# Feed-forward's second product in high and low float32r parts, with identity products in TensorE's waits

## What is computed

```python
s = attention(xn)                       # 16 heads, 4 key groups, rotary, window 64 + front 32
gate, up = split(xn @ ternary(w_gate_up).T)      # 1024 wide each
h = silu(gate) * up
g = silu(rms_norm(h) @ ternary(w_proj).T)        # the second product, 1024 -> 256
x = x + (s @ wo) * g
```

## Time and profile before

| | |
|---|---|
| runs | 811.24 us median of 3 (810.93 to 811.31) |
| the profiled execution | 811.08 us; its span, first to last instruction, 809.3 us |
| TensorE | 769.6 us busy (95%), weight loads 474.5 us (59%) |
| VectorE | 597.1 us busy (74%) |
| ScalarE | 475.9 us busy (59%) |
| GpSimd | 299.7 us busy (37%) |
| line 1044, the second product | 256 records, 59.3 us busy |
| mean granted clock of TensorE | 0.993 |

### The profile page before, as it was taken

How to read it: one execution, slowest core, us unless ns; L and a number is a source line. 1 busy time by engine, 2 the same in 40 slices (tenths; PEclk the granted TensorE clock), 3 DMA queues, 4 the chain that set the end, 5 groups by cost and what they waited for, 6 DMA issues and landing times.

```text
span 809.3 us, 13334 instructions
## 1 busy us (share of the span) xinstructions
PE 769.6 (95%) x4656; PEld 474.5 (59%) x4656; DVE 597.1 (74%) x1584; ACT 475.9 (59%) x968; POOL 299.7 (37%) x255
## 2 busy tenths in 40 slices
PE   4978899899999999999999999999999999999996
PEld 2545578555456667846446667856436667865543
DVE  5989886779766766788856677787948677677852
ACT  3898872536867673243777674143795766233582
POOL 1268770411029882002008885002005887100201
PEclk9999999999999999999999999999999999999998
DMA  9311002381013210084004120057002200027300
GB/s 296 102 58 46 1 29 84 124 232 37 3 33 87 60 33 1 1 260 107 2 14 104 33 64 1 1 164 201 3 2 55 79 21 1 1 78 217 73 3 26
DMA packets 56819, 55.37 MB, mean 68 GB/s; under 512 B 14257, under 2 KB 43313, under 8 KB 56753
## 3 DMA queue, kind: packets, MB, share of 16 engines
q1 hardware_dynamic: 52768, 49.63, 21.5%
q10 hardware_dynamic: 3664, 3.84, 1.8%
q0 software_dynamic: 320, 1.05, 0.4%
HBM read 39.00 MB, written 15.24 MB: 67 GB/s over the span
## 4 chain that ended last, share of the span: by engine, by line
PE 68%; issue 12%; DVE 8%; POOL 5%; ACT 4%; DMA 1%; ACTq 0%; POOLq 0%; DVEq 0%
PE bank L933 13%; PE bank L1044 7%; PE bank L1251 6%; PE bank L1235 5%; PE bank L968 5%; PE bank L1030 5%; PE bank L1146 5%; PE bank L1174 4%; PE bank L1218 3%; PE bank L1011 3%; PE bank L979 2%; PE bank L1223 2%; POOL region L597 2%; PE bank L1166 2%; PE bank L993 2%
## 5 line engine op out<-in xcount | busy, mean ns | idle before, releaser
L1612 DVE TENSOR_REDUCE mx<-bank 128x1 f32<-128x512 f32 x256 | 161.2, 684 | 26.2 <-PE bank L1174 22.7
L601 POOL TENSOR_TENSOR region<-region 128x512 f32<-128x512 f32 x75 | 100.3, 1337 | 148.1 <-DVE region L1429 143.4
L933 PE MATMUL bank<-xnT,wrope 128*128 128x512 f32 x320 | 147.8, 605 | 3.9 <-ACT xnT L728 1.9
L885 ACT ACTIVATE region<-bank 128x512 f32<-128x512 f32 x256 | 132.9, 602 | 25.7 <-PE bank L1223 24.3
L761 ACT ACTIVATE region<-region,nb 128x128 f32<-128x128 f32 x256 | 81.5, 390 | 55.9 <-DVE nb L1441 55.6
L933 PEld LDWEIGHTS bank<-xnT,wrope 128*128 128x128 f32 x320 | 58.8, 194 | 66.6 <-issue 61.8
L597 POOL TENSOR_TENSOR region<-region,sin_sb 128x512 f32<-128x512 f32 x60 | 81.5, 1358 | 41.4 <-ACT region L741 40.8
L630 POOL TENSOR_TENSOR region<-region,bo_bc 128x256 f32<-128x256 f32 x16 | 11.6, 727 | 201.1 <-DVE region L1490 201.1
L1422 DVE TENSOR_TENSOR region<-bank,cos_sb 128x512 f32<-128x512 f32 x80 | 54.3, 686 | 35.2 <-PE bank L933 34.9
L739 ACT ACTIVATE region<-bank 64x512 f32<-64x512 f32 x80 | 47.5, 594 | 49.5 <-DVE region L1422 40.0
L968 PE MATMUL bank<-region 128*128 128x128 f32 x512 | 72.2, 285 | 1.9 <-POOL region L601 1.9
(11 more groups left out here) (148 smaller groups left out, 1336.1 us busy)
## 6 DMA issues: line engine op xcount, KB each, us to landing
wrope<-in_wrope SPq DMA_DIRECT2D x80, 128.0 KB, 2.1
scratch<-region SPq DMA_DIRECT2D x16, 512.0 KB, 4.7
Qp<-scratch SPq DMA_DIRECT2D x56, 128.0 KB, 3.4
Kp<-scratch SPq DMA_DIRECT2D x56, 128.0 KB, 3.8
scratch<-region SPq DMA_DIRECT2D x16, 256.0 KB, 5.2
X<-in_x SPq DMA_DIRECT2D x4, 512.0 KB, 4.1
out<-X SPq DMA_DIRECT2D x16, 128.0 KB, 2.1
VW<-v_rows SPq DMA_DIRECT2D x16, 102.0 KB, 2.8
```

Of the source, the lines that this page charges most:

```text
L601: nc.gpsimd.tensor_tensor(dst, dst, tiles(sw[:, r % 2, :], i), ALU.add)\
L885: nc.scalar.activation(P1[:, n % 8, :], turned_bank(n)[:, :], ACT.Exp, scale=SCALE1)\
L933: mm = nc.tensor.matmul(misc(b, name)[:, 0:width], lhs(c), xnT[:, c, :], start=(c == 0), stop=(c == DC - 1))
L1612: nc.vector.tensor_reduce(mx1[:, g % 2, column:column + 1], scores_bank(m)[:, :], AX.X, ALU.max)\
```

## The change

1. `wpT` is float32r. ScalarE writes each row block of `H` rounded into `H_hi` (in `Qp`'s room), VectorE writes the rest, `H - H_hi`, into `H_lo` (in `Kp`'s room). `projected` does two float32r products of 256 columns in the place of each float32 product.
2. For b of 1 to 3 the gate and up jobs all lie in units 0 to 11; `projected(0)` is done in halves in units 14 and 15, the sums of squares come at the head of step 16, `projected(1)` at its end. `projected(2)` precedes the second `turn_outputs0`, `output0(3)` precedes `turn_half(0)`. For b = 0 `projected(0)` now follows the last probabilities instead of standing in step 16.
3. The root and the gate of tile 0 move to VectorE's steps 16 and 17 for b of 1 to 3; the gate of tile 2 comes before the gated attention of tile 0. The sums have a bank of their own.
4. `keep_busy` turns the identity: 30 times before the first norm is there, 8 times before the first rotary jobs, 8 times in units 7 and 11 of b = 0, 4 times before each `turn_half(0)`, 18 times before the last `wo1` products.
5. Raw weights that lay in `wpT` lie in `H` while they are quantised.

```diff
-FFN_LATER = [0, 0, 2, 2, 0, 0, 2, 2, 0, 0, 2, 2, 2, 1, 1, 0]
+FFN_LATER = [1, 1, 2, 2, 0, 1, 2, 2, 0, 1, 2, 2, 0, 0, 0, 0]
+def ups_at(b, s):
+    return [i for kind, i in ffn_at(b, s) if kind == "up"] if 0 <= s < NKV * TT else []
-        wpT = sb("wpT", [P, HC, DIM])
+        wpT = sb("wpT", [P, HC, DIM], F32R)
+        H_hi, H_lo = Qp, Kp
...
+            def high_rows(b, i):
+                act.wait_ge(h_ready.sem, h_ready.at(b, i + 1))
+                nc.scalar.activation(H_hi[:, i, :], H[:, i, :], ACT.Copy).then_inc(hhi_ready.sem, 1)
...
                     if b == 0 and s:
                         first_blocks(b, s - 1)
+                    for i in ups_at(b, s - 1):
+                        high_rows(b, i)
...
+            def keep_busy(dst, n):
+                for _ in range(n):
+                    nc.tensor.transpose(dst[:, 0:P], ident[:, :], ident[:, :])
             pe.wait_ge(ident_loaded, 16)
+            keep_busy(t_bank[0], FILL_START)
...
+                if h == 0:
+                    keep_busy(misc(b, name), 4)
                 pe.wait_ge(xn_ready.sem, xn_ready.at(b, TT + 2 * h + 2))
...
             turn_rows(0)
+            keep_busy(t_bank[0], FILL_UNIT)
             front(0)
...
-                        mm = nc.tensor.matmul(misc(b, ("proj", t))[:, 0:DIM], H[:, c, t * P:(t + 1) * P],
-                                              wpT[:, c, :], start=(c == 0), stop=(c == HC - 1))
+                        if t == 0:
+                            pe.wait_ge(hlo_ready.sem, hlo_ready.at(b, c + 1))
+                        for part in (H_hi, H_lo):
+                            mm = nc.tensor.matmul(misc(b, ("proj", t))[:, 0:DIM], part[:, c, t * P:(t + 1) * P],
+                                                  wpT[:, c, :], start=(c == 0 and part is H_hi),
+                                                  stop=(c == HC - 1 and part is H_lo))
...
-                    if s == NKV * TT:
-                        pe.wait_ge(h_ready.sem, h_ready.at(b, HC))
-                        projected(0)
+                    if b and s == NKV * TT:
+                        square_sums()
...
+                        if b == 0 and s in FILL_UNITS:
+                            keep_busy(t_bank[(s - 1) % 2], FILL_UNIT)
...
+                        if b and s == OT_UNIT - 1:
+                            projected(0, 0, HC // 2)
                         if s == OT_UNIT:
                             turn_outputs0(b, 0)
+                        if b and s == OT_UNIT:
+                            misc_done(projected(0, HC // 2), ("proj", 0))
                     if 1 <= s <= NKV * TT:
                         turn_probs0(b, s - 1)
                     if s >= 2:
                         attend0(b, s - 2)
+                    if b and s == NKV * TT:
+                        misc_done(projected(1), ("proj", 1))
...
-                misc_done(projected(1), ("proj", 1))
-                turn_outputs0(b, 1)
                 pe.wait_ge(pt1_ready.sem, pt1_ready.at(b, NKV * TT))
                 pe.wait_ge(mx0_done.sem, mx0_done.at(b, NKV * TT * REP))
-                projected(2, 0, 2)
+                if b == 0:
+                    misc_done(projected(0), ("proj", 0))
+                    square_sums()
+                    misc_done(projected(1), ("proj", 1))
+                misc_done(projected(2), ("proj", 2))
+                turn_outputs0(b, 1)
+                projected(3, 0, HC // 4)
                 pe.wait_ge(ot_ready.sem, ot_ready.at(b, 2))
                 output0(0)
                 output0(1)
-                misc_done(projected(2, 2), ("proj", 2))
+                misc_done(projected(3, HC // 4), ("proj", 3))
                 output0(2)
-                misc_done(projected(3), ("proj", 3))
+                output0(3)
                 turn_half(b, 0)
-                output0(3)
...
+                if b + 1 == B:
+                    keep_busy(m_bank[2], FILL_END)
                 pe.wait_ge(y_ready.sem, y_ready.at(b, 2))
...
+            def low_rows1(b, i):
+                dve.wait_ge(hhi_ready.sem, hhi_ready.at(b, i + 1))
+                nc.vector.tensor_tensor(H_lo[:, i, :], H[:, i, :], H_hi[:, i, :], ALU.subtract)\
+                    .then_inc(hlo_ready.sem, 1)
...
                     for kind, i in ffn_at(b, s) if s < NKV * TT else ():
                         (gate if kind == "gate" else times_up)(b, i)
+                    for i in ups_at(b, s - 2) if s < NKV * TT else ():
+                        low_rows1(b, i)
                     if b == 0 and s in SPLIT_LOW:
                         split_ffn1(*SPLIT_LOW[s])
```

More of the change, by code:

```diff
@@ L52 @@
 S16 = SEQ // 32
+FILL_START, FILL_UNIT, FILL_END = 30, 8, 18
+FILL_UNITS = (7, 11)
 class Signal:
@@ L71, in misc_jobs @@
         jobs += [("wt", k) for k in TURN_AT.get(s, ())] if b == 0 else []
-    jobs += [("proj", 0), ("proj", 1), ("ot", 1), ("wo0", 0), ("wo0", 1), ("proj", 2), ("wo0", 2), ("proj", 3)]
-    jobs += [("xh", 0), ("wo0", 3), ("xh", 1), ("v1", 0)] + [("qk", j) for j in range(4)] + [("v1", 1)]
+    jobs += [("proj", 0), ("sum", 0), ("proj", 1), ("proj", 2), ("ot", 1), ("wo0", 0), ("wo0", 1), ("proj", 3)]
+    jobs += [("wo0", 2), ("wo0", 3), ("xh", 0), ("xh", 1), ("v1", 0)] + [("qk", j) for j in range(4)] + [("v1", 1)]
     jobs += [("dup", i) for i in range(HC)] + [("mt", 0)] + [("down", t) for t in range(TT)]
@@ L259, in build @@
         x_slot1 = X[:, 1, :, :].rearrange("p t d -> p (t d)")
-        wp_flat = wpT[:, :, :].rearrange("p c n -> p (c n)")
+        h_flat = H[:, :, :].rearrange("p c n -> p (c n)")
+        h_room = [h_flat[:, n * SEQ:n * SEQ + PIECE] for n in (HC - 3, HC - 5)]
         w0_flat, w1_flat = (w[:, :, :, :].rearrange("p k a b -> p (k a b)") for w in (w0T, w1T))
-        raw_room = [x_slot1, th[:, :, :].rearrange("p t n -> p (t n)"), wp_flat[:, 0:PIECE],
-                    wp_flat[:, PIECE:2 * PIECE], x_slot1, wp_flat[:, 0:PIECE]]
+        raw_room = [x_slot1, th[:, :, :].rearrange("p t n -> p (t n)"), h_room[0],
+                    h_room[1], x_slot1, h_room[0]]
         tern_raw = [raw_room[TERN_ORDER.index(i)] for i in range(NPIECE)]
@@ L402, in released @@
                 "proj": lambda: [(g_ready, n + 1)],
+                "sum": lambda: [(fr_step, 2)],
                 "wo0": lambda: [(sg_step, n + 1)],
@@ L1043, in projected, with square_sums @@
                     for c in range(first, last):
-                        mm = nc.tensor.matmul(misc(b, ("proj", t))[:, 0:DIM], H[:, c, t * P:(t + 1) * P],
-                                              wpT[:, c, :], start=(c == 0), stop=(c == HC - 1))
-                    return mm
+                        if t == 0:
[4 more added lines that the diff above has]
+                                                  stop=(c == HC - 1 and part is H_lo))
+                    return mm
+                def square_sums():
+                    pe.wait_ge(sq_ready.sem, sq_ready.at(b, 1))
+                    misc_take(pe, b, ("sum", 0))
+                    pe.wait_ge(mx0_done.sem, mx0_done.at(b, NT * (NKV * TT - 1)))
+                    for n in range(TT):
+                        mm = nc.tensor.matmul(misc(b, ("sum", 0))[:, n:n + 1], sq[:, 1, n * P:(n + 1) * P],
+                                              ones1[:, :], start=True, stop=True)
+                    misc_done(mm, ("sum", 0))
                 for s in range(NKV * TT + 2):
-                    if s == NKV * TT:
-                        pe.wait_ge(h_ready.sem, h_ready.at(b, HC))
-                        projected(0)
+                    if b and s == NKV * TT:
+                        square_sums()
                     if s < NKV * TT:
@@ L1067, in _ @@
                         attend0(b, s - 2)
+                    if b and s == NKV * TT:
+                        misc_done(projected(1), ("proj", 1))
                     for k in TURN_AT.get(s, ()) if b == 0 else ():
                         turn_weights(k // 2, k % 2)
-                pe.wait_ge(sq_ready.sem, sq_ready.at(b, 1))
-                for n in range(TT):
-                    mm = nc.tensor.matmul(misc(b, ("proj", 0))[:, DIM + n:DIM + n + 1], sq[:, 1, n * P:(n + 1) * P],
-                                          ones1[:, :], start=True, stop=True)
-                misc_done(mm, ("proj", 0))
                 def output0(t):
@@ L1525, in _ @@
                             times_cos(b, r)
+                    for i in ups_at(b, s - 2) if s >= NKV * TT else ():
+                        low_rows1(b, i)
+                    if b and s == NKV * TT:
+                        feedforward_root(b)
                     if b and 1 <= s <= NKV * TT:
@@ L1534, in _ @@
                         (gate if kind == "gate" else times_up)(b, i)
+                    for i in ups_at(b, s - 2) if s < NKV * TT else ():
+                        low_rows1(b, i)
                     if b == 0 and s in SPLIT_LOW:
                         split_ffn1(*SPLIT_LOW[s])
+                    if b and s == NKV * TT + 1:
```

(11 more changed lines are left out.)

14 lines of the change are left out of this document (10 added, 4 removed).

## The result

The changed kernel takes 822.76 us (median of four executions, 821.90 to 823.44) where the kernel before took 811.27 on the same chip (810.93 to 812.79): a ratio of 1.0137, 95% interval 1.012 to 1.0155. It is 1.4% slower; the forecast was 807.7 us, 0.4% faster. The profiled execution took 822.92 us with a span of 821.1, so 11.8 us more span than before.

A forecast was written before the change was run, and what follows sets the result against it. TensorE's work was taken as the bound for b of 1 to 3, a VectorE-ScalarE loop for b = 0. Terms -3.3 + 4.8 - 1.8 - 3.2 = -3.5 us on 811.08 gave 807.6, median 807.7; 8-in-10 range 802.5 to 813.5.

The forecast's parts named there:

- The product's price: Second product on TensorE: a float32r record of 256 columns takes 0.118 us, so `projected` takes 1.89 us instead of 3.45.
- b = 1 to 3 without the low rows: Later sequences: the forecast, which included low rows, was -1.1 us each and -3.3 us for three.
- The stall of 2.0 us: Units 12 and 13, b = 1 to 3: TensorE waits for late maxima and exponentials, 2.0 us (bounds 0.8 and 3).
- the price of the low rows: VectorE's subtractions: 0.85 us each; in b = 0 four in the loop cost 3.4 us, the others and high rows 0.6.
- rival 2: VectorE becomes the bound because its subtractions wait for GpSimd: +6.1 us together, 813.8 us, slower; chance 17%.
- The failed step in b = 0: End of b = 0: last attend to first output grows from 6.10 to 8.2 us, +2.1, as `projected(0)` comes later.
- Start: Up to the first scores: identity turns raise the clock for the first rotary jobs, -1.8 us (bounds 0 and -3.1).
- End: Last product: 18 identity turns keep the clock up, so its 16 records take 3.45 us instead of 6.69, -3.2 us.
- Rival 3: Start and end: identity turns don't hold the clock, those gains vanish, 813.7 us, slower; chance 12%.
- the rule of the Trainium skill: TensorE's clock: a turn does not count as TensorE being busy, and full clock does not engage for it.
- The other cover: High rows on ScalarE: 8 x 0.6 us cost nothing as long as ScalarE idles between exponentials.
- the upper edge: Slow edge of the main forecast's own range, 805 to 810 us (38%), counted as same instead of faster.

The follow-up runs named there:

- e5: The changed kernel without VectorE's low-row subtractions, both passes reading the high rows: 0.9956 of the kernel before.
- e12: The changed kernel with the low row of unit 5 moved to unit 7 of VectorE's list for b of 1 to 3: 1.0104 of the kernel before.
- e15: The changed kernel without the low rows in b = 0 alone, its product reading the high rows twice: 1.0072 of the kernel before.
- e16: The changed kernel without low rows in b = 0 and with that sequence's `projected(0)` back in step 16: 1.0011 of the kernel before.
- e17: The changed kernel with b = 0 in one plain float32 product, old order except `projected(0)` behind all waits: 1.0091 of the kernel before.
- e3: The changed kernel with `projected(0)` of b = 0 put back into step 16, low rows kept: 1.0139 of the kernel before.
- e1: The kernel before with only 30 identity turns at the start and 18 at the end added: 0.9964 of the kernel before.
- e14: The kernel before with only the 18 identity turns at the end added: 0.9968 of the kernel before.
- e10: The changed kernel with b = 0 in one plain product and old order, later low rows on GpSimd, identity turns re-placed: 1.0012 of the kernel before.
- e8: The changed kernel with b = 0 in one plain float32 product, no high or low rows, order of before: 1.0036 of the kernel before.

## Why the prediction was wrong, step by step

**The product's price: right.** 32 records in 3.95 us are 0.123 each with the lead-in, 0.120 from start to start; 0.118 was taken.

**b = 1 to 3 without the low rows: right in sum, by luck in one term.** e5 takes 1.7 us off a sequence where -1.1 was forecast with them. The stall of 2.0 us in the units 12 and 13 was put down to low rows that delay the maxima, ahead of unit 13's turned probabilities. 1.9 came, but 1.07 of it ahead of unit 13's scores, for ScalarE's key copies, and in e5 too. In b = 2 the changed kernel needs 9.31 us from the sums to the end of `output0(1)`, 9.3 forecast; from there to the second `turn_half` 12.60, 11.7 forecast. Of the 0.9 us 0.8 are the clock (0.77 in the window 533.6 to 541): in e5, where it stayed up, it is 11.78.

**The failed step: the price of the low rows.** "Less the overlap with the next one I take 0.85": they took 1.135 on average, 1.05 less an overlap of 0.08 (476.66 + 1.74 against 478.32), past the 0.11 us more from which the text itself let rival 2 decide. That rival named the mechanism, and its size was too small: it put 1.5 on a later sequence beyond the forecast, and 3.1 came (+2.0 for -1.1). It looked for the stalls in units 12 and 13, because the units' cover was thinnest there. The stall came in unit 7, from a row in unit 5 for which I had charged next to nothing (0.2 for banks late in units 7 and 11): 1.3 us a sequence at full clock, by e12. Measured in whole, the low rows cost 14.7 us by the medians: by the traces of the two kernels 3.7 in each middle sequence (0.8 of it clock), and by e15 5.3 in the first, where 3.4 + 0.6 were forecast.

**The failed step in b = 0: the order.** "`projected(0)` no longer lies ahead of it, so this becomes ... +2.1": it counted the product's own time at full clock. It left out that nothing takes the product's place in the wait, and that the wait lowers the clock for what follows. By e16 and e17 the place costs 4.5 to 5.0 us. e3 shows why undoing it alone gives nothing: with the low rows present, the product waits for them in the old place. The two losses hide each other; only e15 and e16 together separate them. A third part of the first sequence was given no term at all: 1.9 us of the start's lead are lost to half clock by unit 5.

**Start: near in number, partly by luck, and wrong in worth.** The first scores came 2.4 us sooner (forecast 1.8), but the trace that this is counted from was late: against e2, the change without turns, it is 0.9. And e1 and e14 agree within their intervals, so the 30 turns alone are worth nothing that shows. In the changed kernel 0.5 us of the lead are left at unit 5, behind the half clock of unit 4 (window 46 to 54: 0.57). In the executions of e5 and e10 unit 4 ran at full clock, and unit 5 starts at 56.5 and 56.7 instead of 58.1. So the lead is not always lost, and what the start's turns are worth in the changed kernel was not tested alone.

**End: right.** -3.0 for -3.2; e2 and e14 confirm it. Rival 3 (turns don't hold the clock) is refuted for the end. No trace here agrees with the rule of the Trainium skill beside it (TensorE: Matmul & The Clock Gate, Part 4: PE-mode transpose). **Norm waits:** with four turns the clock stayed up in the waits of b = 0 and b = 3 and not in b = 1 and b = 2. That the turns held it is not shown: in e2, without them, it stayed up in those of b = 1 to 3 (granted clock 1.00) and fell in b = 0 (window 150 to 154: 0.58). That "TensorE waits over 1 us" there was forecast, that the clock falls was not: 0.8 us in b = 2. **The other cover:** the high rows on ScalarE were put at nothing. No run leaves them out alone, so their price stays open, but they do stand in the way: 0.52 us (507.61 to 508.13) ahead of the key copies that unit 13 waits for, and 1.14 us ahead of e16's product. In e16, where b = 0 has high rows and no low rows, its row turns come at 226.85, in e8, with one plain product, at 226.91: there the high rows and their waits cost what the cheaper product saves.

**The chances:** the parts for slower (17%, 12% and 2%) add up to 0.31, not 0.28; same is 0.19 with the upper edge that makes faster 0.50.

## What to carry to other kernels

An operation added to an engine that is only 70% busy is priced by what stands behind it in that engine's list, not by the idle share: find the consumer that waits (here a bank two units later, for 1.3 of the 3.0 us that the low rows cost a later sequence at full clock) and put the operation after it. Before moving work out of a wait, ask what then fills the wait and at which clock the moved work will run. Turning an identity in the last wait of a program is a cheap gain when the profile shows the last product at half clock; earlier in a program a microsecond won may be lost again at the next wait. And before a difference between two traces is explained, compare it with further traces of programs that are the same up to there: here the first scores of versions without turns at the start lay 1.7 us apart.

## What the runs showed of the hardware

Identity turns on TensorE (float32, 128 x 128) can keep the granted clock up: 18 before the end took the last product from 6.69 us to 3.72, in each of the 17 programs that had them. At the start 30 turns (5.14 us in e1) were followed by 0.52 behind 2.39 us of idle time; with 8 more ahead of the rotary jobs and 1.4 us of idle time these ran at full rate. The clock after a given pattern of waits was not the same in each execution: the same 38 records ran at 1.00 in one and 0.63 in another, and the same 8 records, behind the same program, in 1.16 and 2.08 us. A VectorE subtraction with two SBUF inputs took 0.68 us, and up to 1.78 when it started while a GpSimd operation of the same size was under way, ending some 0.55 us after it; on GpSimd the same operation took 1.36 on average.
